# Logic attention: the left product carries the second values, the last gates come ahead of the first turning, and the left logarithm ahead of the softplus

## What is computed

```python
q1, k1, v1 = _qkv(x, qkv1_w)
q2, k2, v2 = _qkv(x, qkv2_w)
S1 = einsum('bhnd,bhmd->bhnm', q1, k1) * scale
S2 = einsum('bhnd,bhmd->bhnm', q2, k2) * scale
A1, A2 = softmax(S1), softmax(S2)
Cr = log(einsum('bhnk,bhkm->bhnm', A1, A2) + EPS)      # right product
Cl = log(einsum('bhnk,bhkm->bhnm', A2, A1) + EPS)      # left product
feat = stack([S1, S2, S1.T, S2.T, Cr, Cl])
hid = gelu(conv1_w @ feat + conv1_b)                   # 6 -> 16 channels
gates = sigmoid(conv2_w @ hid + conv2_b)               # 16 -> 4 channels
Smix = S1 + g_and*S2 + g_or*(logaddexp(S1, S2) - S1) - g_not*0.5*S2 + g_chain*Cr
y_base = softmax(Smix) @ v1
transport = A2 @ v2
y_chain = A1 @ transport
out = (y_base + sigmoid(chain_logit) * y_chain) @ proj_w
```

## Time and profile before

| what | value |
|---|---|
| median of 3 runs | 2627.47 us (2611.75 to 2633.1) |
| the profiled execution | 2611.67 us, its span 2609.9 us |
| PE, DVE, ACT, POOL busy | 84%, 72%, 62%, 22% of the span |
| loop of logic attention | about 165 to 1370 us of the span |
| mean granted clock of PE | 0.922 of 2.4 GHz |

### The profile page before, as it was taken

One profiled execution on the slowest core, in us unless ns is written; L12 is line 12 of the kernel. 1 busy time (PEld: TensorE's weight loads), 2 busy tenths in 40 slices (PEclk: granted clock), 3 DMA queues, 4 the chain that ended last, 5 costly groups with the idle time before them and its releaser, 6 DMA issues. The chain is left out here.

```text
span 2609.9 us, 55965 instructions
## 1 busy us (share of the span) xinstructions
PE 2198.0 (84%) x22566; PEld 1555.1 (60%) x22566; DVE 1868.2 (72%) x2584; ACT 1619.1 (62%) x2458; POOL 570.5 (22%) x263
## 2 busy tenths in 40 slices
PE   5348999999999999999954958778569999999998
PEld 2135444454444444454323746664459999999998
DVE  0543888888888888888655445673668788888886
ACT  0025888888888888888751314332157777777776
POOL 0023444444444444444210001331000000000000
PEclk9658999999999999999865979999769999999999
DMA  4017777777777777777611000000122222212220
GB/s 172 0 45 199 210 204 213 220 208 218 216 205 206 211 215 217 209 219 216 166 41 41 1 8 3 1 1 21 66 72 77 74 69 69 69 69 74 71 69 34
DMA packets 110228, 306.64 MB, mean 117 GB/s; under 512 B 20334, under 2 KB 56936, under 8 KB 109209
## 3 DMA queue, kind: packets, MB, share of 16 engines
q1 hardware_dynamic: 109977, 303.11, 39.7%
HBM read 170.09 MB, written 80.65 MB: 96 GB/s over the span
## 5 line engine op out<-in xcount | busy, mean ns | idle before, releaser
L579 ACT ACTIVATE la_hid<-ps,la_b 128x904 f32<-128x904 f32 (+1 forms) x480 | 450.8, 988 | 72.6 <-PE ps L434 71.7
L1515 PE MATMUL ps<-ls_xm,ls_w_in_parts 128*128 128x226 f16 x3072 | 467.7, 261 | 13.2 <-DVE ls_xm L1596 9.0
L1523 PE MATMUL ps<-ls_state_parts,ls_w_rec_parts 128*128 128x226 f16 x2976 | 448.0, 259 | 0.0
L1542 ACT ACTIVATE ls_gates<-ps,ls_bias 128x226 f32<-128x226 f32 x768 | 301.6, 446 | 127.0 <-PE ps L1523 126.9
L434 PE MATMUL ps<-la_pairs,la_w 32*64 32x452 f32 x3584 | 311.0, 573 | 45.3 <-ACT la_hid L579 42.4
L1515 PEld LDWEIGHTS ps<-ls_xm,ls_w_in_parts 128*128 128x128 f16 x3072 | 294.5, 97 | 23.1 <-issue 9.3
L1523 PEld LDWEIGHTS ps<-ls_state_parts,ls_w_rec_parts 128*128 128x128 f16 x2976 | 285.2, 96 | 6.3
L447 PE MATMUL ps<-la_hid,la_w 128*32 128x452 f32 x1856 | 248.3, 560 | 1.0 <-ACT la_opened L585 1.0
L408 POOL TENSOR_TENSOR la_P<-la_S,la_top 113x904 f32<-113x904 f32 x64 | 153.3, 2395 | 263.9 <-DVE la_top L682 263.9
L434 PEld LDWEIGHTS ps<-la_pairs,la_w 32*64 32x64 f32 x3584 | 74.3, 131 | 186.4 <-issue 113.0
L396 POOL TENSOR_TENSOR la_P<-la_P,la_inv 113x904 f32<-113x904 f32 x64 | 132.1, 2085 | 189.7 <-DVE la_inv L661 189.7
(11 more groups left out here) (294 smaller groups left out, 4247.8 us busy)
## 6 DMA issues: line engine op xcount, KB each, us to landing
la_pairs<-la_maps SPq DMA_DIRECT2D x224, 452.0 KB, 6.1
la_gate<-la_opened SPq DMA_DIRECT2D x448, 113.0 KB, 3.4
ls_w_all<-ls_weights SPq DMA_DIRECT2D x32, 904.0 KB, 4.1
la_maps<-la_ST SPq DMA_DIRECT2D x32, 791.0 KB
la_maps<-la_S SPq DMA_DIRECT2D x32, 791.0 KB
ls_m_all<-ls_masks SPq DMA_DIRECT2D x32, 456.0 KB, 3.6
la_maps<-la_Cr SPq DMA_DIRECT2D x32, 395.5 KB
la_maps<-la_Cl SPq DMA_DIRECT2D x32, 395.5 KB
```

The source lines that it names most:

```text
L579: act.activation(hid[:, u % 4, 0:n], ps[:, bank:bank + n, 0:HALF], ACT.Gelu_apprx_tanh, bias=b1[:])\
L1515: mm = pe.matmul(out_j, w_in_parts[:, w, e, j, :], xm[:, t % 2, e, :, x, 0:N], start=((w, x) == PASSES[0]), stop=(t == 0 and (w, x) == PAS ...
L1523: mm = pe.matmul(out_j, w_rec_parts[:, w, e, j, :], state_parts[:, x, e], start=False, stop=((w, x) == PASSES[-1]))
L1542: return act.activation(dst, ps[:, n % 3 * 2 + j // 2, j % 2 * 256:j % 2 * 256 + C], ACT.Tanh if j == 3 else ACT.Sigmoid, bias=bias[:, e, ...
```

## The change

The tile `P` (the softmaxes) gets room for 16 more columns behind each head's 113 (PV = 129). DVE's `values` writes the second values there, for the first softmax's half, in place of a tile `V2`. `left_product` multiplies the transposed second softmax by head and values together: one 129-column product per head gives the left product and the transport, so that `transport` and its eight 16-column products are gone. Three heads fit a bank; six lie in banks 0 and 1 (`CA`), two in bank 6 (`X`). What reads them is split in two accordingly: DVE's scaling into `T`, and ACT's logarithm into `Cl`, which now waits until DVE has read `T`'s part of the same banks. On PE, `gates(p, 7)` comes ahead of `turn_softmax(f, 0)`; on ACT the left logarithm comes ahead of `softplus`. `conv(c, 0)` of the next period still waits for `ln_ready`, which the right logarithm and the first part of the left one signal; `chain` and the saving of `Cl` wait for the second part (`tail_logged`).

```diff
+    PV, FIRST = N + DK, 6
...
-        V1, V2 = sb("V1", [N, 5, D]), sb("V2", [N, D])
-        P, PT = sb("P", [N, 2, 2, W]), sb("PT", [N, 2, W])
+        V1 = sb("V1", [N, 5, D])
+        P, PT = sb("P", [N, 2, 2, H, PV]), sb("PT", [N, 2, W])
...
-                                after(pool, s["prod_made"], 2 * (z - 1))
-                            pool.tensor_tensor(by_head(P[:, z % 2, i]), by_head(S[:, z % 4, i]), per_head(top[:, i]),
+                                after(pool, s["tail_made"], z - 1)
...
-                def product(f, i):
-                    pe.wait_ge(s["PT2_out"] if i else s["PT1_out"], f + 1)
+                def right_product(f):
+                    pe.wait_ge(s["PT1_out"], f + 1)
                     for hd in range(H):
-                        mm = pe.matmul(ps[0:N, (CB, CA)[i] + hd // HB, col(hd % HB)], PT[:, i, col(hd)], P[:, f % 2, 1 - i, col(hd)],
+                        mm = pe.matmul(ps[0:N, CB + hd // HB, col(hd % HB)], PT[:, 0, col(hd)], P[:, f % 2, 1, hd, 0:N],
                                        start=True, stop=True)
                     mm.then_inc(s["prod_made"], 1)
+
+                def left_product(f):
+
+
+                    pe.wait_ge(s["PT2_out"], f + 1)
+                    pe.wait_ge(s["V_ready"], f + 1)
+                    for hd in range(H):
+                        bank, at = (CA + hd // 3, hd % 3) if hd < FIRST else (X, hd - FIRST)
+                        mm = pe.matmul(ps[0:N, bank, at * PV:(at + 1) * PV], PT[:, 1, col(hd)], P[:, f % 2, 0, hd, :],
+                                       start=True, stop=True)
+                        if hd == FIRST - 1:
+                            mm.then_inc(s["prod_made"], 1)
+                    mm.then_inc(s["tail_made"], 1)
...
-                def transport(f):
-                    pe.wait_ge(s["V_ready"], f + 1)
-                    pe.wait_ge(s["PT2_out"], f + 1)
-                    for hd in range(H):
-                        d = slice(hd * DK, (hd + 1) * DK)
-                        mm = pe.matmul(ps[0:N, X, d], PT[:, 1, col(hd)], V2[:, d], start=True, stop=True)
-                    mm.then_inc(s["T_made"], 1)
...
-                    if ok(f):
-                        turn_softmax(f, 0)
                     if ok(p):
                         gates(p, 7)
                     if ok(f):
+                        turn_softmax(f, 0)
                         turn_softmax(f, 1)
                         values(f)
-                        product(f, 0)
+                        right_product(f)
                     if ok(e):
                         turn_mix(e)
                     if ok(f):
-                        transport(f)
-                        product(f, 1)
+                        left_product(f)
...
-                def log_product(f, i):
-                    act.wait_ge(s["prod_made"], 2 * f + i + 1)
-                    if i and f >= 1:
+                def log_right(f):
+                    act.wait_ge(s["prod_made"], 2 * f + 1)
+                    act.activation(two(Cr[:, f % 3]), banks(CB), ACT.Ln, bias=tiny[0:N]).then_inc(s["ln_ready"], 1)
+
+                def log_left(f):
+
+                    act.wait_ge(s["T_ready"], 2 * f + 1)
+                    if f >= 1:
                         act.wait_ge(ln_saved[(f - 1) % 2], 64 * ((f - 1) // 2 + 1))
-                    to = Cl[:] if i else Cr[:, f % 3]
-                    act.activation(two(to), banks((CB, CA)[i]), ACT.Ln, bias=tiny[0:N]).then_inc(s["ln_ready"], 1)
+                    x = ps[0:N, CA:CA + 2, 0:3 * PV].rearrange("p k (h n) -> p k h n", n=PV)
+                    act.activation(Cl[:, 0:FIRST * N].rearrange("p (k h n) -> p k h n", k=2, n=N), x[:, :, :, 0:N],
+                                   ACT.Ln, bias=tiny[0:N]).then_inc(s["ln_ready"], 1)
+                    act.wait_ge(s["T_ready"], 2 * f + 2)
+                    x = ps[0:N, X, 0:2 * PV].rearrange("p (h n) -> p h n", n=PV)
+                    act.activation(Cl[:, FIRST * N:W].rearrange("p (h n) -> p h n", n=N), x[:, :, 0:N],
+                                   ACT.Ln, bias=tiny[0:N]).then_inc(s["tail_logged"], 1)
...
-                        log_product(f, 0)
+                        log_right(f)
+                    if ok(f):
+                        log_left(f)
                     if ok(p):
                         softplus(p)
-                    if ok(f):
-                        log_product(f, 1)
...
-                    after(dve, s["T_made"], f)
-                    dve.tensor_copy(V2[:], ps[0:N, X, D:2 * D]).then_inc(s["V_ready"], 1)
+                    after(dve, s["tail_made"], f - 1)
+                    dve.tensor_copy(P[:, f % 2, 0, :, N:PV], ps[0:N, X, D:2 * D].rearrange("p (h d) -> p h d", d=DK)).then_inc(s["V_ready"], 1)
...
-                    dve.wait_ge(s["T_made"], f + 1)
+                    dve.wait_ge(s["prod_made"], 2 * f + 2)
                     after(dve, s["chain_made"], f)
-                    dve.tensor_scalar(T[:], ps[0:N, X, 0:D], w_chain[:], None, ALU.mult).then_inc(s["T_ready"], 1)
+                    dve.tensor_scalar(T[:, 0:FIRST * DK].rearrange("p (k h d) -> p k h d", k=2, d=DK),
+                                      ps[0:N, CA:CA + 2, 0:3 * PV].rearrange("p k (h n) -> p k h n", n=PV)[:, :, :, N:PV],
+                                      w_chain[:], None, ALU.mult).then_inc(s["T_ready"], 1)
+                    dve.wait_ge(s["tail_made"], f + 1)
+                    dve.tensor_scalar(T[:, FIRST * DK:D].rearrange("p (h d) -> p h d", d=DK),
+                                      ps[0:N, X, 0:2 * PV].rearrange("p (h n) -> p h n", n=PV)[:, :, N:PV],
+                                      w_chain[:], None, ALU.mult).then_inc(s["T_ready"], 1)
```

More of the change, by code:

```diff
@@ L269, in logic_attention @@
         names = ("consts_in zeroed act_setup dve_setup qk_made qk_ready S_made half_made S_out ST_out top_ready shifted "
-                 "conv_made hid_ready gate_made opened_ready PT_made PT1_out PT2_out V_made V_ready prod_made ln_ready "
-                 "T_made T_ready chain_made ych_step ych_ready ET_made ET_ready base_made y_step yT_ready out_made added "
+                 "conv_made hid_ready gate_made opened_ready PT_made PT1_out PT2_out V_made V_ready prod_made tail_made ln_ready tail_logged "
+                 "T_ready chain_made ych_step ych_ready ET_made ET_ready base_made y_step yT_ready out_made added "
                  "P_raised sum_step inv_ready P_ready mix_step gates_used two_terms mix_top_step mixed E_raised E_step "
@@ L383, in _ @@
                         sp.wait_ge(s["ln_ready"], 2 * f + 2)
+                        sp.wait_ge(s["tail_logged"], f + 1)
                         save(f, 5, Cl[:].unsqueeze(1), ln_saved)
@@ L394, in _ @@
                         for i in range(2):
-                            x = by_head(P[:, f % 2, i])
+                            x = P[:, f % 2, i, :, 0:N]
                             pool.tensor_tensor(x, x, per_head(inv[:, i * H:(i + 1) * H]), ALU.mult).then_inc(s["P_ready"], 1)
@@ L476, in turn_softmax @@
                     for hd in range(H):
-                        tr = pe.transpose(ps[0:N, (CB, CA)[i] + hd // HB, col(hd % HB)], P[:, f % 2, i, col(hd)], ident[0:N, 0:N])
+                        tr = pe.transpose(ps[0:N, (CB, CA)[i] + hd // HB, col(hd % HB)], P[:, f % 2, i, hd, 0:N], ident[0:N, 0:N])
                     tr.then_inc(s["PT_made"], 1)
@@ L514, in chain @@
                 def chain(b):
-                    pe.wait_ge(s["T_ready"], b + 1)
+                    pe.wait_ge(s["tail_logged"], b + 1)
                     attend(X, T[:], PT[:, 0]).then_inc(s["chain_made"], 1)
@@ L604, in raise_scores @@
                     act.wait_ge(s["shifted"], 2 * z + 2)
-                    x = P[:, z % 2].rearrange("p i w -> p (i w)")
+                    x = P[:, z % 2].rearrange("p i h n -> p (i h) n")[:, :, 0:N]
                     act.activation(x, x, ACT.Exp).then_inc(s["P_raised"], 1)
@@ L657, in sums @@
                     dve.wait_ge(s["P_raised"], f + 1)
-                    signal(dve, dve.tensor_reduce(total[:], P[:, f % 2].rearrange("p i (h m) -> p (i h) m", h=H), AX_X, ALU.add),
+                    signal(dve, dve.tensor_reduce(total[:], P[:, f % 2].rearrange("p i h n -> p (i h) n")[:, :, 0:N], AX_X, ALU.add),
                            s["sum_step"], f + 1)
```

1 line of the change is left out of this document (added).

## The result

The changed kernel takes 2663.18 us (median of 6 runs, 2651.61 to 2671.2) against 2625.44 us for the kernel before (6 runs, 2611.75 to 2633.1): ratio 1.0152, 95% interval 1.011 to 1.0194. It is slower by 1.5%, and the prediction (2616.4 us, 2597 to 2641) is wrong. The profiled execution took 2651.61 us, its span 2649.8 us. Every ratio in this document leaves out runs that lie over 1.5% above the fastest of their kernel; the only one is e8's of 2667.9 us.

A forecast was written before the change was run, and what follows sets the result against it. ACT was taken as the path in the period's tail. 0.71 us in each of 30 periods plus 2.6 gave 23.9 us less; 12.8 for falls left 11.1, so 2616.4 us against the median, range 2597 to 2641.

The forecast's parts named there:

- the count of falls: Drops of PE's clock to half behind its longer wait, over the loop: 4 taken, none and 30 the ends; cost 12.8 us.
- rival 2: PE's new wait drops the clock in most periods, slower: 15 falls give 2651.6 us, all 30 2699.6; chance 0.17.
- PE's wait ahead of the second convolution step: PE's idle time behind the chain, until the first gelu: grows from 0.77 to 1.97 us in every period.
- A fall: PE's clock dropping to 1.2 GHz behind the wait: four steps each 0.8 us longer, 3.2 us.
- The gates' move: Last gates ahead of the first turning on PE: ACT's copy comes earlier, gaining 0.89 us a period on the path.
- The split logarithm: ACT's left logarithm in two parts ahead of the softplus: costs 0.18 us a period.
- The clean period: A steady loop period where the clock stays up: 34.15 us, against 34.86 before.
- rival 1: Clock stays up after PE's 1.97 us wait, no falls: 23.9 us less, 2603.6 us; chance 0.20.
- T in time: DVE's first part of T is ready before ACT's left logarithm, with 0.65 us to spare.
- The joined product on PE: Transport's 1.52 us go, the wider left product costs 0.21 more; off the path in steady periods.
- Rival 3: Gain eaten by another wait, on DVE's T, the strided exponential or the gates' DMA: about 2622 us; chance 0.18.
- The filling periods: Two periods that fill the pipeline, PE's products on the path: gain 1.3 us each, 2.6 together.

The follow-up runs named there:

- e8: Changed kernel with one unused product put into PE's wait behind the chain in each period; 2647.07 us, ratio 1.0091 to the kernel before.
- e5: Changed kernel with the softplus ahead of the left logarithm again; 2618.29 us, ratio 0.9977 to the kernel before.
- e13: Changed kernel with nine unused products behind the chain in the period of image 12 alone; 2653.49 us, ratio 1.0125 to the kernel before.
- e1: Changed kernel with four unused products put into PE's wait behind the chain in each period; 2592.97 us, ratio 0.989 to the kernel before.
- e3: Kernel before with only the last gates moved ahead of the first turning; 2598.24 us, ratio 0.9902 to the kernel before.
- e2: Changed kernel with the last gates put back between the two turnings; 2685.5 us, ratio 1.0229 to the kernel before.
- e11: Kernel before with the joined product alone, plus two unused products behind the chain; 2616.34 us, ratio 0.9986 to the kernel before.
- e4: Changed kernel with the output and projection moved behind the next period's first convolution step and the chain; 2638.52 us, ratio 1.0052 to the kernel before.
- e7: Changed kernel with two unused products behind the chain in each period; 2583.8 us, ratio 0.985 to the kernel before.
- e10: Same kernel as e7 run again, the changed kernel with two unused products behind the chain; 2582.65 us, ratio 0.986 to the kernel before.
- e6: Kernel before with the joined product alone, gates and softplus in their old places; 2678.02 us, ratio 1.0218 to the kernel before.

## Why the prediction was wrong

- **The step that failed is the count of falls**, "I take 4". Measured: 20 in the steady window, and 24 from 265 to 1303 us. It rested on two rows, a wait of 1.64 us without a fall and one of 2.47 with, between which I interpolated. e8 shows falls after 1.43 us, e5 after 0.87 and 1.12 us together, and e8 and e13 show clean periods after the very same waits. A single wait that did no harm said nothing about one that comes 30 times.
- **The mechanism and rival 2 were right**, though the forecast did not follow them. PE's wait ahead of the second convolution step was predicted at 1.97 us and measured at 2.05. A fall was priced at 3.2 us; a fallen period is 37.54 us against 34.03, 3.5 us. With 24 falls the prediction's own sum against the profiled execution is 2611.7 - 23.9 + 24 x 3.2 = 2664.6; the profiled execution took 2651.6. Of these 13 us, 1.2 lie ahead of the first opening (238.7 us in place of 242.5, where 2.6 of gain were forecast) and 1.7 behind the last. The other 10.1 lie between the two, where the long fall of before has no counterpart; it had made a period of 39.5 us (1245.84 to 1285.38) in place of 34.86. e1 shows the cause: with the wait filled, the time falls by 2.6% against the changed kernel (0.989 over 1.0152).
- **The gates' move**: predicted 0.89 us on the path, measured 0.99 (e3). The opening waits 1.04 us and no longer 2.10, and the copy follows with no gap, since the turning was in time. e2's clean periods are 35.02 us against the changed kernel's 34.03, the same 0.99.
- **The split logarithm**: predicted 0.18 us, measured 0.15 (765.56 to 767.67 is 2.11 against 1.96), and 0.17 from e11 (35.03 against 34.86).
- **The clean period** is 34.03 us; 34.15 was predicted. Without falls the sum was -23.9 us (rival 1); e1 is 28 us below the kernel before, with an interval of 14 to 44 that holds 23.9.
- **T in time**: predicted 0.65 us to spare. DVE's first part ends at 764.87 and the logarithm starts at 765.56, 0.69 us. The rows of DVE:

```profile
763.58 1.06 DVE L759 COPY la_ET<-ps 113x904 f32<-113x904 f32 x1
764.56 0.31 DVE L764 TENSOR_SCALAR la_T<-ps,la_w_chain 113x96 f32<-113x96 f32 x1
```

- **The joined product on PE**: its row is 0.12 us longer (1.94 against 1.82) where I took 0.21. None of PE's 2 us was on the path, as predicted; e11 shows that the joined product is worth nothing even with the clock kept up.
- **Rival 3** is absent from the changed kernel (ACT waited for the gates' DMA once, 3.0 us) but shows in e3, 22.3 us in 13 waits, and in e4, 45.0 us in 26.
- **The filling periods** were to gain 2.6 us, and they did gain. They lie ahead of the first convolution. In the twelve profiled executions with the joined product the first opening stands at 238.5 to 241.7 us, in the four without it at 242.5 to 244.8. From the loop's first projection (at 164.62 us before, 164.88 in the changed kernel) to the first scores of the third of its periods the changed kernel is 1.4 us quicker (44.74 against 46.10), where 1.3 a period were forecast. To the first convolution that waits for a gelu it is 4.1 us quicker (67.00 against 71.12), and part of that is the clock: over 211 to 226 us it is 0.55 where it was 0.50, and over 226 to 235 us 1.00 where it was 0.91. PE's timeline before, then changed:

```profile
210.72 2.27 PE L469 MATMUL ps<-la_q,la_k 32*113 32x113 f32 x16 [3.53 <-DVE la_ych L667]
...
235.74 1.80 PE L434 MATMUL ps<-la_pairs,la_w 32*64 32x452 f32 x16 [0.78 <-ACT la_hid L579]
```

```profile
209.62 1.36 PE L471 MATMUL ps<-la_q,la_k 32*113 32x113 f32 x16 [3.18 <-DVE la_ych L682]
...
231.88 1.80 PE L436 MATMUL ps<-la_pairs,la_w 32*64 32x452 f32 x16 [1.12 <-ACT la_hid L584]
```

- **The first falls** come right behind the filling periods: the changed kernel's PE waits 2.06 us and takes 2.60 us for the convolutions at 265.07, and again 2.59 us at 302.55. The row at 302.29 of the earlier trace rows stands in that period (image 2, the third with convolutions), where the kernel before had its harmless wait of 1.64 us.

The chance of 0.17 for falls in most periods was too low by the prediction's own evidence: the only long wait in the steady rows was 0.77 us, and every row above that came once. The Trainium skill, "TensorE: Matmul & The Clock Gate", section "HAM oscillation", describes the clock dropping anew at each pass of a loop with waits between bursts. The waits of its loop are of some 3 to 5 us; this trace shows the same drop in 20 consecutive periods behind 2.05 us. By that, the recurrence deserved more weight than one occurrence of 1.64 us.

## What to carry to other kernels

When an engine that is off the critical path gets faster, its work turns into one longer wait, and on PE that wait can cost more than the work did: 2 us taken out of PE's tail cost up to 3.5 us in each of two dozen periods here. Before shortening PE's work beside a path on another engine, write down where its idle time will stand and how long it is with its neighbours, and treat it as harmless only if waits as long recur in the steady loop with the clock up. If the change is wanted, a few unused products in the wait give the clock back (two of them, 2582.65 us). Here the gates' move alone already gives nearly all of the loop's gain without them: from the first opening to the last it is 1095.1 us before, 1065.0 in e3 and 1063.2 in e1 and e7.

## What the runs showed of the hardware

- A repeated wait of PE of 2.05 us was followed by 10.2 us at 1.2 GHz in each of 20 consecutive periods, and one of 1.43 us (e8) in each period from 780 us on, though PE was 84% busy over the span and, in the stretch shown, busy for 10.13 us of the 10.20. A wait of 0.99 us was followed by a fall in one period each of e7 and e10.
- The falls of the changed kernel and of e8 keep step: once begun they come in every period, now 37.5 us long, after 5 clean periods (changed kernel) or 13 (e8) with the same wait. In e2 and e6, with clean periods of 35.02 us, they came in 20 of some 26. A period with nine fillers, which delayed the loop once by 1.2 us, was followed by three periods without falls.
- Two waits of 0.87 and 1.12 us, 1.5 us apart, did what one longer wait does; waits of 1.23 and 0.77 us with 2.8 us of work between them (e4) didn't.
- Unused work on PE made the changed kernel faster by 2.6% (e1).
- Behind the loop the same kernel (e7, e10) ran 50 us of unchanged code at a granted clock of 0.80 in one execution and 0.53 in another, and the stretch behind the last opening took 1278.1 and 1288.9 us.
